# Second attention of a two-layer graph kernel: column maxima 28 tiles ahead instead of 24, the offsets' store at step 6 and their load at step 11

## The reference, cut to what is computed

```python
adj = jnp.maximum(adjacency_matrix, eye)
q = jnp.einsum('nd,hdk->hnk', node_matrix, Wqs)
k = jnp.einsum('nd,hdk->hnk', node_matrix, Wks)
v = jnp.einsum('nd,hdk->hnk', node_matrix, Wvs)
scores = jnp.einsum('hqk,hmk->hqm', q, k) * kd ** (-0.5)
scores = scores + IDENTITY_BIAS * eye - MASK_VAL * (1.0 - adj)
att = jax.nn.softmax(scores, axis=-1)
return jnp.einsum('hqm,hmk,hko->qo', att, v, Wo)
...
x = _layernorm(x + _L0_gnn_ref(x, adj, ...), axis=-1)
x = _layernorm(x + _L1_gnn_ref(x, adj, ...), axis=-1)
```

## Time and profile before

| | |
|---|---|
| Median of 3 runs | 4965.33 us (4965.26 to 4973.84) |
| The profiled execution, its time | 4967.11 us |
| Its span | 4965.3 us |
| Mean granted PE clock of the span | 0.927 |
| Busy: PE, DVE, ACT, POOL | 84%, 73%, 73%, 7% |
| Second attention, first to last exp | 2566.3 to 4778.3 us |
| From 2566 to 4780, of 2214 us: PE, DVE, ACT busy | 2118.7, 1901.6, 2078.5 us |
| Idle of ACT before the exp, put down to the offsets' store | 85.6 us in 13 times, 49.8 of it before the loop |

### The profile page before, as it was taken

The page is one execution under the profiler, slowest core; times in us unless marked ns, Lnnn a source line. Parts: engine busy times, 40 slices in busy tenths (PEclk is TensorE's granted clock), DMA queues, the critical chain, the costliest instruction groups (busy, mean ns, idle before and its releaser), DMA issues. The chain is left out here.

```text
span 4965.3 us, 106706 instructions
## 1 busy us (share of the span) xinstructions
PE 4163.5 (84%) x42500; PEld 2761.3 (56%) x42500; DVE 3641.2 (73%) x6026; ACT 3633.4 (73%) x4642; POOL 343.2 (7%) x527
## 2 busy tenths in 40 slices
PE   7922239988998999699749999999999999999977
PEld 4412228888888898444315555555555555555543
DVE  1245559999999999622258888888888888888834
ACT  1133349999999999411139999999999999999952
POOL 0000000000000000000010202011120202111000
PEclk9955559999999999899969999999999999999999
DMA  1299994444444444344453635444353535444223
GB/s 63 86 305 362 355 339 148 162 165 152 149 162 162 155 149 161 105 149 156 138 140 91 167 87 143 103 126 122 93 164 86 160 88 147 111 116 130 68 72 144
DMA packets 413632, 742.27 MB, mean 149 GB/s; under 512 B 90040, under 2 KB 282744, under 8 KB 376184
## 3 DMA queue, kind: packets, MB, share of 16 engines
q1 hardware_dynamic: 349296, 643.60, 43.0%
q0 software_dynamic: 20608, 75.51, 4.7%
q10 hardware_dynamic: 43280, 16.92, 1.3%
HBM read 567.42 MB, written 168.49 MB: 148 GB/s over the span
## 5 line engine op out<-in xcount | busy, mean ns | idle before, releaser
L1186 DVE CUSTOM_DVE_ANT_0 m_junk<-m_rough,m_rows 128x1024 bf16<-128x1024 f32 x1024 | 1253.6, 1224 | 304.7 <-PE m_rough L1053 236.7
L671 PE MATMUL g_acc<-g_vals,g_pos 128*128 128x130 f16 (+1 forms) x8192 | 1201.1, 250 | 128.7 <-DVE g_neg L626 102.0
L552 ACT ACTIVATE g_step<-g_arow,g_steep 128x512 bf16<-128x512 f32 x2048 | 1258.4, 711 | 58.5 <-DVE g_neg L626 38.2
L1135 ACT ACTIVATE m_scores<-m_strip 128x1024 f32<-128x1024 bf16 x1024 | 1053.0, 1028 | 103.4 <-POOL m_strip L984 39.7
L1149 ACT ACTIVATE m_whole<-m_scores 128x1024 int32<-128x1024 f32 x1024 | 1037.7, 1013 | 83.9 <-DMA scr_offset<-m_offset 35.8
L1067 PE MATMUL m_acc<-m_v,m_halves 128*128 128x129 f16 (+1 forms) x16384 | 901.8, 208 | 49.4 <-ACT m_got L1112 49.4
L671 PEld LDWEIGHTS g_acc<-g_vals,g_pos 128*128 128x128 bf16 x8192 | 811.5, 99 | 207.0 <-DVE g_neg L626 104.4
L1067 PEld LDWEIGHTS m_acc<-m_v,m_halves 128*128 128x128 f16 x16384 | 754.9, 98 | 286.4 <-issue 189.8
L1081 PE MATMUL m_scores<-m_qA,m_kA 128*128 128x512 f16 x2048 | 786.2, 384 | 33.1 <-ACT m_scores L1135 33.0
L1086 PE MATMUL m_scores<-m_qB,m_kB 65*128 65x512 f16 x2048 | 784.9, 383 | 0.0
L1211 DVE TENSOR_SCALAR m_halves<-m_whole 128x2048 f16<-128x2048 uint16 x1024 | 708.6, 692 | 80.2 <-ACT m_whole L1149 73.1
(11 more groups left out here) (146 smaller groups left out, 3161.3 us busy)
## 6 DMA issues: line engine op xcount, KB each, us to landing
g_vals<-scr_gat_v SPq DMA_DIRECT2D x128, 1040.0 KB, 5.3
m_v<-scr_v SPq DMA_DIRECT2D x64, 1032.0 KB, 7.3
b_stage<-in_adj SPq DMA_DIRECT2D x64, 1024.0 KB, 9.8
m_kA<-scr_k_hi SPq DMA_DIRECT2D x128, 512.0 KB, 6.1
scr_row_mask<-b_rowm SPq DMA_DIRECT2D x64, 512.0 KB, 8.7
scr_no_edge_T<-b_colm SPq DMA_DIRECT2D x64, 512.0 KB, 8.3
g_strip<-scr_no_edge_T SPq DMA_DIRECT2D x64, 512.0 KB, 7.6
m_kB<-scr_k_lo SPq DMA_DIRECT2D x64, 512.0 KB, 5.4
```

Of the source, the lines that this page charges most:

```text
L552: ins = nc.scalar.activation(step[:, j % RING, t, :], arow[:, b, :], ACT.Sigmoid, scale=STEEP, bias=steep[:, b, 2 * j + t:2 * j + t + 1])
L671: mm = pe.matmul(acc[:, b, it, lo:hi], edges, vals[:, b, 2 * j + t, lo:hi], start=j == 0 and t == 0 and lo == 0, stop=j == PAIRS - 1 and t ...
L1135: nc.scalar.activation(scores[:, n % 2], strip[:, 2 * st:2 * st + 2, :].rearrange("p t i -> p (t i)"), ACT.Copy, scale=-BIG / 2).then_inc( ...
L1186: nc.vector.tensor_tensor_reduce(out=junk[:, n % 2], in0=rough[:].rearrange("p a m -> p (a m)"), in1=rows[:, n % TC, n // TC * WIDE:(n // ...
```

## The change

EARLY goes from 24 to 28. The offsets' store moves from step 10 to step 6 and their load from step 12 to step 11. POOL reloads four pieces of the rows, not two, in the unit with u mod 8 = 5, and the other four, not six, in the next.

```diff
--- before.py
+++ after.py
@@ -874,7 +874,7 @@
     STEPS, ERING, SLOTS, KSLOTS, TILES, LAG = NT // 2, 4, 3, 4, TC * N // WIDE, 3
     ROWS_B = F + 1
     VW = VA + F + 1
-    EARLY = 24
+    EARLY = 28
     assert TILES == STEPS
     with ExitStack() as ctx:
         s = Space(nc, ctx, "m")
@@ -1028,9 +1028,9 @@
                 c = u // H + 1
                 if c < C:
                     if u % H == H - 3:
-                        reload_rows(c, range(2))
+                        reload_rows(c, range(4))
                     if u % H == H - 2:
-                        reload_rows(c, range(2, PIECES))
+                        reload_rows(c, range(4, PIECES))
                     if u % H == H - 1:
                         reload_strip(c)
 
@@ -1139,9 +1139,9 @@
                 for st in range(STEPS):
                     if st == 10 and not first:
                         store(u - 1)
-                    if st == 10 and u + 1 < U:
+                    if st == 6 and u + 1 < U:
                         store_offset(u + 1)
-                    if st == 12 and u + 1 < U:
+                    if st == 11 and u + 1 < U:
                         load_offset(u + 1)
                     act.wait_ge(scored, STEPS * u + st + 1)
                     if not (first and st < 2):
```

## The result

The changed kernel takes 4913.53 us in the median of 5 runs (4910.55 to 4919.68), the kernel before 4965.26 (4960.44 to 4973.84). The ratio is 0.9898 with a 95% interval of 0.9884 to 0.9911: 1.0% or some 51 us faster. The forecast was 4925 with 4918 to 4945 as its range. On a second chip the same kernel had the ratio 0.9898 (0.9882 to 0.9915) again; its medians there, 4927.02 and 4973.21, lie 46 us apart, so the gain is better read as 46 to 52 us than as 51.7.

The account below looks back on a forecast made before the run. The prediction took ACT to bound the second attention, its waits for the offsets' store paid in full. 4967.1 (profiled) - 50.6 + 8.4 + 2 = 4926.9, forecast as 4925 because the median is 1.8 lower; range 4918 to 4945.

Parts of the forecast that it names:

- ACT sets the pace: Second attention: two activations a step leave ACT nothing to spare, so whatever holds its queue is paid in full.
- Four tiles before the loop: Before the first step: four more rough tiles at 2.10 us each, +8.4 us in full on the path.
- gain 50.6: Chunk changes, units with u mod 8 = 6 and 7: all ACT waits for the offsets' landing go, 50.6 us.
- I keep 2: Waits left over at the chunk changes: 2 us kept, bounded by nothing and 20.
- 54.1 us of this stage are disturbance: Exps of the second attention: 2212.0 us where 2157.9 would do; saving ACT's waits can give no more than 54.1.
- Reduction and offset to DVE's step 4: DVE, moved from step 8 into 0.86 us of idle time: cost nothing; without that cover 21 us on DVE.
- The rows' pieces at 0: POOL's reload, pieces 2 and 3 a unit earlier: cost 0; late pieces would make DVE and PE wait.
- The load one step earlier at 0: Offsets' load at step 11: 9.9 us before PE needs it, landing bounded by 2.6 to 9.9, cost 0.
- Sum: Whole kernel: 4967.1 profiled - 50.6 + 8.4 + 2 = 4926.9; forecast 4925 for the median.
- Rival 1: Units like 14 and 15: store and load meet POOL's transfers, so ACT or PE waits; 4943 us, chance 0.22.
- Rival 2: ACT still waits though the store landed, or landings stretch; gain under 18, 4955 to 4975 us, chance 0.05.
- Rival 3: ACT's step 6: DVE's offset comes late for the store in every unit; 4988 at 1 us each, chance 0.05.

Follow-up runs that it names:

- c1_before_divide6: The kernel before with the division moved on DVE from step 8 to step 6: 4970.30 us beside 4973.21, ratio 1.0001.
- f1: The kernel before with the offsets' load at step 14, the output's store at step 12 and DVE's division at step 6: ratio 0.9895.
- f2: The kernel before with the offsets' load at step 14 and the output's store at step 12: ratio 0.9892.
- a2_before_out11: The kernel before with the output's store moved from step 10 to step 11: 4952.36 us, ratio 0.9949.
- b4: The kernel before with the offsets' load at step 14 instead of 12: 4919.24 us beside 4960.33, ratio 0.9915.
- a1_early_only: The changed kernel with the offsets' store back at step 10 and their load at step 12: 4962.17 us beside 4975.89 before, ratio 0.9968.
- a3_load8: The changed kernel with the offsets' load at step 8, two steps behind their store: 4947.39 us, ratio 0.9949.

## Why the prediction was wrong in size, point by point

- **ACT sets the pace; its waits are paid in full, with what follows them.** Right. The excess of the pairs was 50.6 and is gone to the last microsecond (-51.1).
- **Four tiles before the loop, +8.4.** Right: 91.1 against 84.0 in the two profiles is 7.1, most likely because DVE's three waits for the first rows were 1.4 shorter in the later one (54.7 against 56.1); 7.1 + 1.4 = 8.5. Over all profiles the stretch is 81.5 to 84.0 with 24 tiles and 90.2 to 92.3 with 28.
- **"gain 50.6", less "I keep 2", and "54.1 us of this stage are disturbance, and nothing that saves ACT's waits can give more".** This step failed: the gain of the stage stood in the sum at 48.6, with 54.1 as its bound, and the exps gained 57.6. Of the 9.0 between, 2 were kept for a remainder that did not come, 0.5 lies in the pairs, 4.9 in the 47 other units, which the sum had put at nothing (the bound allows them 3.5), and 1.6 in unit 0 and the last two. The undisturbed unit by which I measured, 33.75, was itself not free: DVE's step 8, with reduction, division and offset, cost 0.07 a unit (c1_before_divide6; f1 against f2), and two stores issued behind each other in ACT's step 10 delayed six exps by 0.6 to 1.0 (gone in a2_before_out11). The change parts both pairs as a side effect. How the 4.9 divides between them is open: c1_before_divide6 and f2 against b4 give 3.4 and 1.6, the way over a1_early_only (1588.5) gives 1.3 and 3.6. The means by step would have shown a cost there: step 9 took 2.23 in the mean before and 2.06 after, the steps around it 2.00 to 2.09.
- **How much of this repeats.** The 4.9 does: the 47 units take 1584.2 to 1585.0 in all six profiles with the offset made at step 4 or 6 and no second issue in ACT's step 10. The 1.6 does not: in the second profile of the changed kernel unit 0 and the last two took 1.8 more than before, and the exps gained 53.6 in all, within the bound of 54.1. So the unit of 33.75 was too long a floor, but only by 0.03 in the mean (1584.9 over 47 is 33.72), some 1 to 2 us in all.
- **Reduction and offset to DVE's step 4 at nothing.** Right, and better than nothing. DVE stood idle for 0.78 before that maximum after the change too, with the reduction in the gap:

```profile
2609.46 0.17 DVE L1193 TENSOR_REDUCE m_cmax<-m_most 128x4 f32<-128x16 f32 x1
2610.40 1.23 DVE L1186 CUSTOM_DVE_ANT_0 m_junk<-m_rough,m_rows 128x1024 bf16<-128x1024 f32 x1 [0.78 <-PE m_rough L1053]
...
2611.55 0.17 DVE L1197 TENSOR_SCALAR m_offset<-m_cmax 128x4 f16<-128x4 f32 x1
```

- **The rows' pieces at 0.** Right for the change as a whole, but only because of its own lines: with the old split they cost 29.9 in the one profile, some 21 by the ratios.
- **The load one step earlier at 0.** Right: no late load in either profile. The bound behind it, "Even the upper one just fits", was no bound: a load of a2_before_out11 took 10.3 against the 9.9 of room. The 2 us of fixed cost that I set beside it from the Trainium skill (DMA: Bandwidth & Descriptors, Anatomy of one DMA) are given there for DMAs that GPSIMD (POOL in the rows) issues; this load and the store are issued by ACT, so the 9.9 is no test of that figure.
- **Sum.** 40.2 foretold against the profiled execution, 54.2 found: 7.0 in the exps (0.5 pairs, 4.9 other units, 1.6 ends), 2 kept, 5.1 chance in the stages before, and 1.3 and 1.4 that cancel (prologue, last exp to the end). The median fell out of the range partly by luck: 4965.3 - 57.6 + 8.4 = 4916.1 by the first profile is still under my 4918, but 4965.3 - 53.6 + 8.4 = 4920.1 by the second is inside. The low end stood on the failed step, and had no room for what executions differ by. The upper end of my narrower range was added up wrongly as well: 7 left over, of which 2 are kept already, is 4930 and not 4932.
- **Rival 1** (the transfers are met elsewhere) did not come. Its worst landing at step 6 was 8.8, and 10.3 lay between. By the Trainium skill (DMA: Bandwidth & Descriptors, Issuing engines are not separate DMA queues) the store interleaves with pieces issued after it; the runs agree so far that a3_load8 waits among just those pieces, its landings up to 8.6, but the store is not held until all have drained: in unit 14 of the changed kernel it went out at 3051.23 and landed 7.1 later, while the last of the four pieces landed some 4 us behind it. **Rival 2** named rightly that one cause might be misread: not in the sum, but in the split. I had put all to the gap, and a1_early_only shows 17 of the 50.6 that the moved pieces take away without it, while b4_before_load14 shows 46.6 that the gap takes away without them. The two overlap: either alone takes the units with 6 from 15.7 to -0.2. **Rival 3** (the offset late at step 6) did not come: the offset was made at 2611.7, ACT's store went out at 2612.94.

## What to carry to other kernels

A transfer that an in-order engine stores and loads back should have its two ends as far apart in that queue as its consumer allows, measured by the longest landing at the busiest moment, not by the median, and the load's own landing counts too; here one line that moved the load two steps gave nearly what the larger change did, without its prologue. Count what a change takes out of crowded steps besides the wait that it aims at, from the mean duration of each step over many units, and don't take a typical quiet unit of the old schedule for a floor. Where work runs further ahead, look up who refills its inputs: the refill has to move by as much.

## What the runs showed of the hardware that I had not expected

- On ACT's queue the issue of a 1 KB store of 128 pieces took 0.33 us alone, 0.52 directly behind another store, and 1.01 to 1.46 in 7 of 63 units in the kernel before (in a1_early_only ten took 0.83 to 1.57). That can delay the activation behind it (six exps before, eleven in a1_early_only), and the wait is then put down to an engine that had long been done.
- A small store behind a 128 KB store of the same queue landed in 3.7 us in the median and 9.9 at most (the kernel before), ahead of it in 3.2 and 8.5 (a2_before_out11).
- The load of 1 KB was in time with 3.9 us of room in 62 of 63 units (b4_before_load14), while the store of the same kilobyte took up to 9.9. Of the late ones the longest in two other kernels took 6.4 (f1_load14_out12_div6, 4189.53 - 4183.15) and 10.3 (a2_before_out11), both behind the 128 KB store of the same queue and beside the strip's pieces.
